# Shared network four half groups earlier, first maxima and shared weights made among the last expert tiles

## What is computed

```python
xn = layernorm(x)
# attention: 16 heads of 16, projections of rank 32
q, k, v = heads(holo(xn, q)), heads(holo(xn, k)), heads(holo(xn, v))
a = softmax(q @ k.T * 0.25) @ v
y1 = holo(a, o)
# mixture of 8 experts, the best 2 for each token, hidden size 352
combine = top2(softmax(xn @ gate_w.T)) normalised * 2.5
y2 = sum_e combine[:, e] * ((silu(xn @ wg[e]) * (xn @ wu[e])) @ wd[e])
# shared network, hidden size 704
y3 = (silu(xn @ sw_gate) * (xn @ sw_up)) @ sw_down
out = x + y1 + y2 + y3
```

## Time and profile before

| | |
|---|---|
| median of 3 runs | 979.91 us (979.81 to 980.3) |
| the profiled execution | 981.48 us, its span 979.7 us |
| TensorE matmul busy | 878.4 us, 90% |
| VectorE busy | 611.4 us, 62% |
| ScalarE busy | 582.2 us, 59% |
| GpSimd busy | 400.7 us, 41% |
| mean granted TensorE clock | 0.949 |

### The profile page before, as it was taken

One profiled execution on the slowest core, in us unless ns is written; L12 is line 12 of the kernel. 1 busy time (PEld: TensorE's weight loads), 2 busy tenths in 40 slices (PEclk: granted clock), 3 DMA queues, 4 the chain that ended last, 5 costly groups with the idle time before them and its releaser, 6 DMA issues.

```text
span 979.7 us, 19365 instructions
## 1 busy us (share of the span) xinstructions
PE 878.4 (90%) x6423; PEld 608.5 (62%) x6424; DVE 611.4 (62%) x923; ACT 582.2 (59%) x932; POOL 400.7 (41%) x384
## 2 busy tenths in 40 slices
PE   4745999999999985788999998999998999999998
PEld 3425999999999982244644644645644645645546
DVE  7777844434434446576786686786786686787642
ACT  5745744444444441477677577677677577677673
POOL 2002622222222203247357356356366356366463
PEclk9865999999999995699999999999999999999999
DMA  9983756222222314356656656667566567564220
GB/s 308 388 249 118 240 143 176 67 75 75 64 75 69 71 57 135 115 132 169 199 144 199 184 149 190 186 155 211 168 154 201 159 154 213 166 161 121 73 83 22
DMA packets 90951, 147.35 MB, mean 150 GB/s; under 512 B 17433, under 2 KB 51745, under 8 KB 88065
## 3 DMA queue, kind: packets, MB, share of 16 engines
q1 hardware_dynamic: 84192, 128.58, 44.5%
q0 software_dynamic: 6480, 17.70, 6.5%
q10 hardware_dynamic: 208, 0.14, 0.1%
HBM read 86.58 MB, written 54.71 MB: 144 GB/s over the span
## 4 chain that ended last, share of the span: by engine, by line
PE 61%; DMA 15%; DVE 14%; SPq 4%; issue 3%; ACT 2%; POOL 1%; ACTq 0%; POOLq 0%; DVEq 0%
PE bank L1438 8%; PE bank L1294 8%; PE s_pair L1276 7%; PE st_pair L1276 7%; DVE top L1874 7%; PE s_pair L1353 6%; PE bank L1402 5%; PE bank L1515 5%; DMA xT_b<-xn_T_split 5%; DMA q_rows<-top_T 4%; PE st_pair L1426 4%; PE bank L1284 2%; PE bank L1259 2%; DMA low_rank_rows<-ro 2%; SPq L632 1%
## 5 line engine op out<-in xcount | busy, mean ns | idle before, releaser
L1874 DVE TENSOR_REDUCE top<-s_pair 128x2 f32<-128x1024 f32 x252 | 308.7, 1225 | 159.9 <-PE s_pair L1353 159.4
L1065 ACT ACTIVATE prob<-st_pair 128x1024 f32<-128x1024 f32 x256 | 262.7, 1026 | 119.1 <-PE st_pair L1426 118.0
L750 POOL DMA_INDIRECT xg<-xn_rows,token_of x71 | 78.9, 1111 | 224.6 <-PE bank L1259 168.9
L1402 PE MATMUL bank<-xT_b,w_sh 64*128 64x512 f32 x960 | 142.5, 401 | 1.0 <-DVE ro L1943 0.2
L1353 PE MATMUL s_pair<-k_rows,q_rows 48*128 48x512 f32 x504 | 121.7, 477 | 20.3 <-DVE top L1874 19.1
L1438 PE MATMUL bank<-prob,v_ones 128*32 128x512 f32 x1024 | 126.4, 612 | 0.0
L1426 PE MATMUL st_pair<-q_rows,k_rows 50*128 50x512 f32 x512 | 110.2, 425 | 17.4 <-DMA q_rows<-top_T 12.9
L796 POOL DMA_INDIRECT y_b<-expert_rows,slot_of x64 | 63.0, 984 | 148.5 <-PE st_pair L1426 141.8
L1402 PEld LDWEIGHTS bank<-xT_b,w_sh 64*128 64x128 f32 x960 | 91.2, 185 | 30.5 <-issue 7.6
L1353 PEld LDWEIGHTS s_pair<-k_rows,q_rows 48*128 48x128 f32 x504 | 49.3, 190 | 77.0 <-DVE top L1874 65.0
L1294 PE MATMUL bank<-w_exp,c_hT 128*128 (+1 forms) x639 | 94.2, 292 | 1.0 <-ACT c_y L985 1.0
(11 more groups left out here) (234 smaller groups left out, 1201.5 us busy)
## 6 DMA issues: line engine op xcount, KB each, us to landing
xT_b<-xn_T_split SPq DMA_DIRECT2D x14, 1024.0 KB, 7.5
qk_rows<-qk_hi SPq DMA_DIRECT2D x56, 256.0 KB
q_rows<-qk_rows SPq DMA_DIRECT2D x64, 192.0 KB
k_rows<-qk_rows SPq DMA_DIRECT2D x56, 192.0 KB
expert_rows<-c_y SPq DMA_DIRECT2D x71, 128.0 KB, 1.7
xn_T_split<-x_T SPq DMA_DIRECT2D x8, 1024.0 KB, 6.4
qk_rows<-qk_lo SPq DMA_DIRECT2D x28, 256.0 KB
x_all<-in_L_attn_x_dram SPq DMA_DIRECT2D x8, 512.0 KB, 8.3
```

The source lines that it names most:

```text
L750: pool.indirect_dma_start(xg[s % 4][:, :], None, xn_dram, bass.IndirectOffsetOnAxis(token_of[:, s:s + 1], 0)).then_inc(c_x[s % 4], 16)
L1065: act.activation(prob[n % 3][:, 2 * jp:2 * jp + 2, :].rearrange("p j l -> p (j l)"), st_pair[:, :], ACT.Exp, scale=HD ** -0.5).then_inc(a_ ...
L1402: ins = pe.matmul((g_bank, u_bank)[up][:, :], w_sh[rows, a, o:o + P], for_shared(b)[rows, c, k, :], start=(n == 0 and i == 0), stop=(n == ...
L1874: dve.tensor_reduce(top[g % 2][:, :, jp, qt], score_pair(b, g, v)[:, :].rearrange("p (i k) -> p i k", i=2), AX_X, ALU.max).then_inc(d_max, 1)
```

## The change

The units of the shared network are shifted: `SHIFT = 2` puts the first two gate-up units of batch b + 1 into group 3 of batch b, units 2 to 4 and the odd one into groups 0 and 1, and the two down units into group 2. The odd piece is now the last of the six (`BOTH = SFT - 1`, no more `ORDER`). `slot(-1, 2)` is gone; the 8 scores and maxima of group 0, the split, the low-rank rows of batch 1 and `turn_max(0, 0)` stand among and behind the last 7 tiles, which use one pair of banks for gate and up. The shared weights are made in four pieces each, on ScalarE after tiles 64 to 67, on GpSimd behind the last four gathers. `xT_b` of a batch is loaded once, in front of the queue of group 2. `o_b` has two buffers and is loaded at the end of group 3 for the next batch; `y_b` is halved and each quarter is added at once. In the last group `score_T` uses both pairs in turn. After the last slot only the attention output is left.

```diff
-        FIRST = 2
-        ORDER = (0, SFT - 1) + tuple(range(1, SFT - 1))
-        BOTH = 1
+        SHIFT = 2
+        BOTH = SFT - 1
...
-            c, j = b if u >= FIRST else b - 1, (u - FIRST) % 8
+            c, j = (b if u + SHIFT < 8 else b + 1), (u + SHIFT) % 8
...
-            slot(-1, 2)
             slot(-1, 3)
...
+        def score_T_pair(b, g, t):
+            return s_pair if (b, g) == (LAST, 3) and t % 2 else st_pair
...
+        LATER = FULL - 4
+        def gu_bank_of(s, i):
+            return gu_bank[0 if isinstance(s, int) and s >= LATER else i % 2]
...
+            def shared_low(i):
+                wait(pool, c_d, LATER)
+                wait(pool, s_hi, i + 1)
+                part = slice(i * S_PIECE, (i + 1) * S_PIECE)
+                pool.tensor_tensor(w_sh[:, LO, part], s_raw[:, part], w_sh[:, HI, part].bitcast(F32), ALU.subtract).then_inc(s_lo, 1)
+
             for s in range(NS):
                 gather(s)
-            pool.wait_ge(s_hi, 1)
-            pool.wait_ge(d_m, 1)
-            pool.tensor_tensor(w_sh[:, LO, :], s_raw[:, :], w_sh[:, HI, :].bitcast(F32), ALU.subtract).then_inc(s_lo, 1)
-            pool.wait_ge(s_lo, 1)
+                if s >= NS - SH_PIECES:
+                    shared_low(s - NS + SH_PIECES)
...
+            def shared_high(i):
+                if i == 0:
+                    act.wait_ge(s_in, 112)
+                part = slice(i * S_PIECE, (i + 1) * S_PIECE)
+                act.activation(w_sh[:, HI, part], s_raw[:, part], ACT.Copy).then_inc(s_hi, 1)
...
+            for s in range(LATER, NS):
+                step(s, s % 4, last=s == NS - 1)
+                if s < LATER + SH_PIECES:
+                    shared_high(s - LATER)
...
 # TensorE, the last seven tiles
                     gate_up(s + i, i, at[i + 2])
+                    if last:
+                        if i == 0:
+                            pe.wait_ge(c_hk, LATER)
+                        score(0, 0, i)
...
                     down(NS - 2, END - 2, at[run])
+                    score(0, 0, run)
+                    low_rank(1)
                     down(NS - 1, END - 1, at[run + 1])
+                    turn_max(0, 0)
...
 # SyncE
+            for s in range(LATER, NS):
+                store_y(s, s % 4)
+                if s == 66:
+                    load_xT(1)
...
+                if g == 2 and there(b + 2):
+                    load_xT(b + 2)
                 if ppg % 2 and moved(ppb, ppg // 2):
                     load_inverse(ppb, ppg // 2)
-                if g == 3 and there(b):
-                    load_x_b(b)
...
-                if g == 2 and there(b + 2):
-                    load_xT(b + 2)
...
-                if g == 3 and there(b) and there(b + 1):
-                    load_xF(b + 1)
...
+                if g == 3 and there(b + 1):
+                    load_x_b(b + 1)
...
 # TensorE, behind the last slot
             slots(slot)
+            low_rank_o(LAST, (0,))
             values(LAST, 3, TPB - 2)
             values(LAST, 3, TPB - 1)
-            down_shared(LAST, 0, range(9))
             turn_last_o(1)
-            down_shared(LAST, 0, range(9, 17))
             turn_back(1)
-            low_rank_o(LAST, (0,))
-            down_shared(LAST, 1)
             low_rank_o(LAST, (1,))
-            down_shared(LAST, 2)
             project_o(LAST, 0)
             project_o(LAST, 1)
-            down_shared(LAST, 3)
```

More of the change, by code:

```diff
@@ L244, in build_program @@
         h_T = sb("h_T", [P, 2, SFT, L], F32R, late)
-        y_b = sb("y_b", [P, TPB, 2, D], F32, late)
-        o_b = sb("o_b", [P, TPB, D], F32, late)
+        y_b = sb("y_b", [P, 2, 2, D], F32, late)
+        o_b = [sb(f"o_b{i}", [P, TPB, D], F32, late) for i in range(2)]
         r_rows[0] = sb("r_rows0", [96, 3, L], F32R, late)
@@ L250, in build_program @@
         xT_b = sb("xT_b", [P, 2, KT, L], F32R, late)
+        top = [sb(f"top{i}", [P, 2, 2, TPB], F32, late) for i in range(2)]
+        top_parts = [sb(f"top_parts{i}", [P, 2, 2, 2, TPB], F32R, late) for i in range(2)]
+        top_T = [sb(f"top_T{i}", [32, P], F32R, late) for i in range(2)]
         xT_bs = [xT_b, xT_1]
@@ L1088, in last_o_high @@
                 wait(act, b_res, LAST)
[L1089 removed]
+                act.activation(ao_T[rows, HI, 1, :], m_bank[rows, :], ACT.Copy).then_inc(a_bo, 1)
             def slot(b, g):
@@ L1097, in slot @@
                         up_half(c, q)
-                    if t == 5 and there(nb):
+                    if t == 5 and there(nb) and now:
                         max_rows(nb, ng)
@@ L1116, in slot @@
                         qk_high(b + 1, PROJECTED.index((g, t)))
-                    if g == 3 and t == 2 and there(b + 2):
+                    if g == 3 and t == 2 and there(b + 2) and now:
                         low_rank_high(b + 2)
@@ L1271, in gate_up @@
                 for n, (free, done) in enumerate(((c_sl, c_g), (c_hk, c_u))):
-                    wait(pe, free, s - 1)
+                    wait(pe, free, s if isinstance(s, int) and s > LATER else s - 1)
                     for m, (a, c) in enumerate(PRODUCTS):
@@ L1616, in slot @@
                         values(b, g, 1)
-                    if t == 4 and there(nb):
+                    if t == 4 and there(nb) and now:
                         turn_max(nb, ng)
@@ L1854, in _ @@
                     low_part(s + 3)
-            with dve.Fori(2, NS // 4) as s4:
-                for i in range(4):
-                    step(s4 * 4 + i, i)
-            for i in range(END):
-                step(FULL + i, i, last=True)
-            h_out(NS - 1, END - 1)
-            dve.wait_ge(c_yk, NS)
             def qk_low(b, n):
@@ L1948, in slot @@
                     if t < STEPS - AHEAD:
-                        if there(nb):
+                        if there(nb) and now:
                             maximum(nb, ng, t + AHEAD)
@@ L1952, in slot @@
                         maximum(qb, qg, t - STEPS + AHEAD)
-                    if t == STEPS - AHEAD - 1 and there(nb):
+                    if t == STEPS - AHEAD - 1 and there(nb) and now:
                         split_max(nb, ng)
@@ L1968, in slot @@
                         qk_low(b + 1, PROJECTED.index((g, t - 1)))
-                    if g == 3 and t == 3 and there(b + 2):
+                    if g == 3 and t == 3 and there(b + 2) and now:
                         low_rank_low(b + 2)
```

322 lines of the change are left out of this document (154 added, 168 removed).

## The result

The changed kernel takes 993.34 us (989.53 to 1005.88, 4 runs) where the kernel before takes 980.11 (979.81 to 981.3): a ratio of 1.0095, 95% interval 1.0053 to 1.0137. The execution of 1005.88 us was a slow one and is not in the ratio, which is therefore not the quotient of the two medians. The kernel is slower by about 1%, where I forecast 962. The profiled execution took 991.98, with a span of 990.2 us.

| stretch | before | after | difference | forecast |
|---|---|---|---|---|
| (a) to the end of the last tile's down product | 363.7 | 372.2 | +8.6 | +6.0 |
| (b) from there to the first transposed scores | 24.4 | 16.5 | -7.9 | -8.9 |
| (c) batch 0 | 76.3 | 73.1 | -3.2 | -4.2 |
| (d) batches 1 to 6 | 431.1 | 452.6 | **+21.4** | -3 |
| (e) batch 7, groups 0 to 2 | 50.9 | 51.7 | +0.8 | +0.6 |

A forecast was written before the change was run, and what follows sets the result against it. TensorE was taken as the limit in batches 1 to 6, with both ends of stage 3 shortenable. Terms 6.0 - 8.9 - 4.2 - 3 + 0.6 - 5.5 - 3.0 = -18.0 gave span 961.7, median 962 us, range 953 to 972.

The forecast's parts named there:

- (a): Last seven tiles, with score pairs and low parts set among them: +6.0 us, bounds +4 and +9.
- (b): From the last tile to batch 0, filled with two gate-up units: -8.9 us, bounds -11 and -2.
- (c): Batch 0, with units from the start and TensorE warm: -4.2 us, bounds -6 and -1.
- (d): Batches 1 to 6, same units in another order with fewer DMA waits: -3 us, bounds -9 and +8.
- (e): Batch 7, groups 0 to 2, two gate-up units become two down units: +0.6 us, bounds -1 and +2.6.
- Edits at nothing: Addition in quarters and halved y_b on GpSimd, taken as free; some 0.5 us a batch if the cover went.
- cold ends: Rival, chance 0.2: clock stays low from the last tile into batch 0 and through the tail; about 971 us.
- (f): Last group, without units, set by ScalarE: 8.5 us between first and last transposed scores, -5.5, bounds -6.2 and -4.
- (g): Last transposed scores to the end: 16.2 us with a partly lower clock against 19.2, -3.0, bounds -5 and -1.
- Sums behind the activations: Rival, chance 0.05: the sums' move waits behind the 1 MB load, VectorE stands in group 2; 983 at 3.5 us a batch.
- Free middle: Rival, chance 0.1: waits of batches 1 to 6 go almost wholly, -9 us, and the tiles have no stall; 953.

The follow-up runs named there:

- e1: Changed kernel with GpSimd making the hidden product of unit 4 and its low part ahead of a sum and a gather in group 1: 979.76 us.
- e10: Kernel before the change, with two sums of y placed directly ahead of the hidden product of unit 0 in group 1: 1003.98 us.
- e7: e1 with the next batch's first two gathers of y issued at steps 0 and 1 of group 3 instead of 4 and 6: 978.71 us.
- e2: Changed kernel with the first two gathers of y moved from group 3 to group 0, the others behind them: 1017.38 us.
- e5: e1 with gathers spread from group 0 step 2 to group 2 step 0 and sums of y behind the hidden products due: 968.64 us.
- e9: e5 with the last group's transposed scores all in one pair of banks, as before the change: 975.56 us.
- e11: e5 with the 1 MB activation load back behind the other DMAs of group 2: 969.92 us.
- e6: e5 with the four low parts of the shared weights made behind all gathers: 967.45 us.
- e3: e2 with the edit of e1 as well: 1018.89 us.
- e12: e6 with the rows of the later group issued behind the low-rank load in group 3: 978.32 us.

## Why the prediction was wrong, point by point

**The step that failed is (d), batches 1 to 6: -3 forecast, +21.4 measured**, beyond its upper bound of +8. The gain side was nearly right (5.4 us of the old waits went, half of 13.7 forecast); the cost side was not. I had put down against the gain only SyncE's queue and VectorE's chain, and let GpSimd pass under "Edits at nothing": "GpSimd, which has 229 of 431 us busy", some 0.5 us a batch if the cover went. That is the mistake. A busy share says that the work fits into the batch; it does not say that a product of 1.28 us which ScalarE and then TensorE need at once comes in time, when 3.5 us of sums and 1.03 us of a gather's issue stand ahead of it in one list. Shifting the units moved all products of GpSimd by two half groups against its sums and gathers, so every place in its list had to be worked out anew: when each input comes, what stands in front, who is waiting behind. I did that for no entry of it. In the medians the first of these places cost 13.6 us (e1), and in the old layout a larger fault of the same kind cost 20.7 us of the middle by itself (e10).

The second half of the same omission is the two gathers that were moved into group 3, in front of the load of the low-rank rows: 9.3 us of waits for `r_rows`, which go when the gathers stand elsewhere (e7, e2, e5). The second gather is issued 1.1 us before the load (608.03 and 609.09). That the load is late because both use the same DMA engines fits the times; I have not shown it by itself. The Trainium skill, "Trainium Kernel Development and Optimization", Key Constraints, says that DMAs issued from different engines' queues run on the same 16 DMA engines and interleave; the load's 8.2 us against 6.1 agree with that, without proving it.

**Why it costs more than the waits.** 12.3 us of the 21.4 are idle time, 9.1 the lower clock behind it. I counted the clock in (b), (c) and (g), and not in the middle, because the middle had 1.00. The Trainium skill, "TensorE: Matmul & The Clock Gate", Part 1, says that activity releases the throttled state; the windows show the other direction: 1.24 us busy of 2.70, and then 6.9 us at 1.2 GHz.

**(a)**, +6.0 forecast, +8.6 measured, inside its bounds. The stall is where and nearly what I said (rows of the profile after, the last tiles in order of time):

```profile
342.64 2.54 POOL L763 TENSOR_TENSOR w_sh<-raw_all,w_sh 128x1088 fp32r<-128x1088 f32 x1 [14.51 <-PE bank L1308]
...
345.32 0.96 POOL L755 DMA_INDIRECT xg<-xn_rows,token_of  x1
...
349.01 0.49 PE L1273 MATMUL bank<-ident_f,xg 128*128 128x128 f32 x2 [2.34 <-DMA xg<-xn_rows,token_of]
...
349.21 3.74 PE L1290 MATMUL s_pair<-w_exp,xg_T 128*128 x12
```

The wait is 2.34 us, 2.2 forecast. Two sizes were off. A tile with a score pair takes 4.15 us where it took 3.57, so a pair costs 0.58, not 0.36, 1.5 us over seven. And the stall lowers the clock: the 12 products of gate and up right behind it took 3.74 us, those of the tile before 2.16.

**(b)**, -8.9 forecast, -7.9 measured. Into batch 0, after:

```profile
374.01 0.27 PE L1378 MATMUL bank<-ident_f,top_parts 128*32 128x128 f32 x1 [1.77 <-DVE ro L1898]
...
374.39 3.39 PE L1409 MATMUL bank<-xT_b,w_sh 64*128 64x512 f32 x24
...
380.02 0.80 PE L1363 MATMUL s_pair<-k_rows,q_rows 48*128 48x512 f32 x2 [2.24 <-DMA q_rows<-qk_rows]
...
388.71 0.40 PE L1437 MATMUL st_pair<-q_rows,k_rows 50*128 50x512 f32 x2
```

The idle time before the turn (2.1 forecast, 1.77) and unit 0 (3.3 forecast, 3.39) were right. I missed the load of group 1's rows, issued only at 373.91 and waited for at 380.02 for 2.24 us, between the two units; behind it the clock was at its lower level until 386.8. This is also part of *cold ends*: both ends were half warm (0.79 here, 0.91 at the end), which is what the forecast took. **(c)**, -4.2 forecast, -3.2 measured, with a clock of 0.95.

**(e)** was right. **(f)** was nearly so, 9.3 us against 8.5, and e9 shows that the missing units alone do not make it: the second pair of banks is needed. I had put both in one sentence; two pairs with the units kept was not tried. **(g)**, -4.4 measured: it took 14.9 us, the 15 of my chain, and the 1.2 us that I added for a falling clock were not needed, since the granted clock stayed at its upper level to 987.6 with TensorE busy for 6.6 us of 14.9. The end of that chain, after:

```profile
985.57 0.51 PE L1531 MATMUL s_pair<-w_rows,ro 96*128 96x256 f32 x2 [1.41 <-DVE ro L1934]
...
986.72 0.68 DVE L1909 TENSOR_TENSOR o_b<-st_pair,o_b 128x512 f32<-128x512 f32 x1
```

**The rivals.** *Sums behind the activations*, which I held to be the only way to a slower kernel, did not happen: VectorE waits for no DMA in the middle. In batch 2 the move of the sums is issued at 576.71, 2.6 us behind the load of 1 MB, and VectorE inverts them at 586.59 without a wait for them; e11 says the same from the other side. *Free middle* was half right, but only in e5, whose middle is 4.5 us shorter than before. The rival that came true, GpSimd's order, was not on my list, and it was to be had from the trace of before: 98.2 us of GpSimd's waits there end with a transposed score that allows a gather, and its list is tied to steps of the groups throughout.

**What the experiments point to.** e5 and e6 beat both kernels: 968.64 and 967.45 us, 1.1 to 1.4% under before. Of the 18 us forecast by span, e5 has 17.2 in its quickest execution; of the medians it has some 13, since its slower executions reach 978.

## What to carry to other kernels

When units of work are shifted against the rest, write out every engine's list around them, also that of an engine that is half idle: for each entry the time at which its input comes, what stands ahead of it, and who waits behind it. Short products that another engine needs at once go ahead of long work that nobody waits for; the same instructions in a wrong order cost 24 us of 980 in the old kernel (e10, medians), and the right order gave back 25 us of 993 in the new one (e5). Then look at the asynchronous transfers that moved along with the entries, and price a stall on TensorE with the clock that it may take with it: here 12.3 us of idle time cost 21.4 us in all, 1.7 times as much. After an edit of the order, do it again for what moved: e2 and e3 cured the wait that I looked at and made a worse one.

## What the runs showed of the hardware

I had not expected the clock to fall in a stretch in which TensorE is busy for 93% of the time. It did so seven times in the changed kernel (27.3 us in all), at or behind waits of 1.2 to 2.3 us, and six times in e10, behind waits of 1.2 to 2.9; in e5, with waits of at most 1.7 us in the middle, it fell once there (675.1, 3.4 us). The length of the wait alone does not decide it: the kernel before has waits of 2.18 and 1.71 us at 464.40 and 608.89 and no low-clock stretch in its middle.

How much the clock falls differs between executions of one kernel, and the time goes with it: the four of the changed kernel took 989.53, 991.98, 994.69 and 1005.88 us at mean granted clocks of 0.953, 0.950, 0.947 and 0.933, and the four of e5 964.35, 966.32, 970.95 and 978.13 us at 0.961, 0.964, 0.958 and 0.949. That the kernels with more stalls spread more is not shown: the kernel before stayed within 0.2% beside the changed one, but went from 977.0 to 987.7 us, 1.1%, in the 23 executions beside e9 to e12.

A load of three DMAs, with two gathers of GpSimd issued shortly before it, was followed by its first use after 7.1 to 8.2 us in the changed kernel, where TensorE waited for it each time, and after 5.7 to 6.0 us, with no wait, in e7, which issues the gathers earlier; a small move issued 2.6 us behind a load of 1 MB came in time for a use 9.9 us later.
